# Attention with pooled levels, then eight gated experts, on one core: unit 0's operands built in place by TensorE, pooling by TensorE, and the experts' weights split during units 4 to 6

## The chip, the cores and the metric

One NeuronCore of a Trainium2 chip runs the whole program. The number that counts is the device time in microseconds (us) of one launch, median of the runs; it is compared with the kernel before on the same chip. Engines are named PE (TensorE), DVE (VectorE), ACT (ScalarE), POOL (GpSimd) and SP (SyncE, which here only issues DMAs).

## The reference, cut to what matters

```python
# x: (B=2, T=1024, C=128); 16 heads of 8; windows of 64 keys; 4 levels of 8 pooled keys
x = x + attention(layernorm(x)) @ W_proj + b_proj
#   qkv = xn @ W_attn + b_attn;  per head: scores against the last 64 keys, and, at each level l,
#   against 8 keys that are means over 8*2^l positions of the block of 64*2^l before;
#   mn = min over the five groups of (max over the group's scores); exp(S - mn);
#   the pooled terms are weighted by 8*2^l; sum over all; divide
x = x + moe(layernorm(x))
#   8 experts: h = x @ W1[e].T + b1[e] (512 wide);  g = h[:256] * sigmoid(h[256:]);  eo = g @ Wo.T + bo
#   out = sum over the two chosen experts of eo * gate
```

## The kernel before

All engines walk one list of steps, `SCHEDULE`, written by `schedule()`; each engine issues, in that order, its part of each step, and semaphores tie them. So a wait on one engine holds back all that stands behind it on that engine, and on no other.

**Units.** Attention runs in eight units (2 batches times 4 groups of 4 heads). A unit has ten slots ("score", u, i): slots 0 and 1 are the scores against pooled keys (8 small matmuls each, 64 columns), slots 2 to 9 those against the window (two matmuls of 256 columns, in two of the eight slots a third of 512 columns that adds the mask). ACT takes the exponent of each slot, DVE masks it, and PE multiplies it into the values in the step "out", three slots later. Between them stand the steps of `beside`: work for the other batch, or for the second part of the kernel.

**The maxima.** exp needs the minimum over the groups of the maxima first. The kernel bounds it by the pooled scores: step "guard" (two times 4 matmuls) computes them, "shift" reduces them and splits the negative shift in two parts, "shiftT" transposes it, and "shift load" sends it by two DMAs from ACT's queue into rows 96 to 103 of `qst` and rows 96 and 97 of `qmk`, from where it takes part in the score matmuls as additional rows. "score" slot 0 waits for both.

**Stacked operands.** q and k are computed in fp32r as a rounded part and a rest (`split3`: hi times hi, hi times lo, lo times hi). One unit's `qst` holds 96 rows (three slots of the group's 32 rows: hi, hi, lo), `kst` the keys (hi, lo, hi), `qmk` the queries masked by head, `pkm` the pooled keys masked by head. They are stacked by DMAs: unit 0 from SBUF (`load_queries(0)`, `load_pooled(0)`, `load_keys(0)`, `load_head_queries(0)`), the later ones from a copy of q, k and the pooled keys in DRAM, which the spills write (`spill_queries`, `spill_pooled`, `spill_keys`). Pooling: DVE sums x over 8, 16, 32 and 64 positions into `xpool`, splits it, and "kp" and "pv" multiply it by the weights; "pv" is moved into `vpool` by 8 instructions of DVE and 8 of ACT. Head columns of `pkm` for unit 0 are made by ACT and DVE from `pks`.

**Experts.** `w1` of each expert (512 KB) is loaded to a staging buffer (three of them), summed by POOL (`whole_w1`), rounded by ACT into `w1T_hi` (the buffer of `qmk[0]`) and its rest written by DVE into `w1T_lo`. All eight "w1" steps stand in unit 7. After unit 7 come 16 x 8 steps "hidden" of three 512-column matmuls each, which end the kernel.

**Keeping PE's clock.** `IDLE` names places at which PE multiplies a buffer of zeros, `still`, to stay busy while it would wait.

Of the kernel before, what the change touches and what calls it, by code (L numbers as in the profile page):

```python
# [42 lines left out]
P = 128  # L43
# [23 lines left out]
C_POOLW = C_BAND + WIN  # L67
C_DEN = C_POOLW + 1
# [1220 lines left out]
```

## Time and profile before

| what | value |
|---|---|
| median of 3 runs | 306.48 us (305.94 to 309.51) |
| the profiled execution's own time | 304.07 us |
| its span in the profile | 301.8 us |
| PE / DVE / ACT / POOL busy | 91% / 63% / 53% / 43% |
| mean granted clock of TensorE | 0.876 of 2.4 GHz |
| stages (first score of each unit on PE) | unit 0 at 37.5 us, 1 at 61.9, 2 at 83.2, 4 at 117.5, 7 at 161.5, experts from 187.7 |

The stages partition the span, since PE runs through all of them. "PEclk" of a stretch is the mean of the granted clock: 1.00 is 2.4 GHz, 0.50 is 1.2 GHz, a value between is a stretch with both. A fp32 matmul shows as two instructions in the trace, a fp32r one as one.

### The profile page before, as it was taken

Reading aid. Unit: us, or ns where it says so; the run is one execution under the profiler, and the core shown is the slowest. Engines: PE = TensorE matmul, PEld = TensorE weight load, DVE = VectorE, ACT = ScalarE, POOL = GpSimd, SP = SyncE. Lnnn points to the kernel's source line nnn. Section 1 sums busy time; section 2 is a strip of 40 time slices with the busy share of each in tenths; the row PEclk is TensorE's granted clock in tenths of the full one; section 3 lists DMA queues with packets and bytes.
Section 4 is the critical chain, followed back from the end, with each engine's and each line's share of the span. In section 5 each row is a group of like instructions: output and inputs, shape, how many; then the busy total and the mean of one; then the engine's idle time right before and its main releaser. Section 6 shows DMA issues by size and latency. Waiting matters only on the chain.

```text
span 301.8 us, 6664 instructions
## 1 busy us (share of the span) xinstructions
PE 275.2 (91%) x2380; PEld 226.4 (75%) x2380; DVE 189.7 (63%) x515; ACT 159.5 (53%) x325; POOL 130.5 (43%) x217
## 2 busy tenths in 40 slices
PE   8673789579999899999999997999999999999994
PEld 6452688378788789887888876768888777888883
DVE  7953447705774641544754478677877888778773
ACT  8629262122655637663376374734485655555551
POOL 6200103501312010211250791487788388888882
PEclk9997665755899669999899558999999999999999
DMA  7137765322177654444225670100000000000000
GB/s 223 40 87 239 246 206 131 94 62 38 28 258 240 219 145 118 97 125 102 54 75 157 219 213 21 28 0 18 11 9 11 2 9 18 10 11 9 17 11 17
DMA packets 25215, 27.30 MB, mean 90 GB/s; under 512 B 13056, under 2 KB 19328, under 8 KB 25184
## 3 DMA queue, kind: packets, MB, share of 16 engines
q1 hardware_dynamic: 23840, 25.85, 29.6%
q10 hardware_dynamic: 1344, 1.05, 1.3%
q8 instruction: 19, 0.31, 0.4%
q14 instruction: 12, 0.10, 0.1%
HBM read 15.81 MB, written 7.86 MB: 78 GB/s over the span
## 4 chain that ended last, share of the span: by engine, by line
PE 69%; DVE 10%; ACT 8%; DMA 7%; issue 2%; POOL 1%; SPq 1%; ACTq 1%; DVEq 0%
PE bank L1102 12%; PE bank L1104 11%; PE bank L1103 11%; PE bank L1248 10%; PE bank L1230 6%; PE bank L1218 4%; DMA qmk<-nshiftT 4%; PE bank L1156 3%; DMA w_stage<-w 3%; PE bank L1205 2%; PE bank L1251 2%; PE bank L1227 2%; ACT vpool L426 2%; DVE arena L1058 2%; PE bank L1171 2%
## 5 line engine op out<-in xcount | busy, mean ns | idle before, releaser
L702 POOL TENSOR_TENSOR work<-work 128x256 f32<-128x256 f32 x110 | 80.7, 738 | 27.1 <-DVE work L1085 14.5
L1085 DVE SCALAR_TENSOR_TENSOR work<-bank,comb,work 128x256 f32<-128x256 f32 x128 | 59.2, 481 | 24.8 <-ACT work L834 23.3
L834 ACT ACTIVATE work<-bank 128x256 f32<-128x256 f32 x128 | 48.3, 384 | 44.8 <-PE bank L1104 44.5
L809 ACT ACTIVATE work<-bank 128x512 f32<-128x512 f32 x64 | 37.1, 594 | 39.2 <-PE bank L1230 36.6
L645 POOL COPY vaug<-vwin 128x64 f32<-128x64 f32 x64 | 18.4, 332 | 80.6 <-PE bank L1251 74.5
L1248 PE MATMUL bank<-work,vaug 128*36 128x64 f32 x1024 | 49.7, 251 | 2.7 <-DVE work L1032 2.7
L1248 PEld LDWEIGHTS bank<-work,vaug 128*36 128x36 f32 x1024 | 38.2, 132 | 13.1 <-DVE work L1032 3.8
L1032 DVE TENSOR_TENSOR work<-work,const 128x512 f32<-128x512 f32 x48 | 33.8, 709 | 11.3 <-ACT work L809 11.2
L1230 PE MATMUL bank<-qmk,kst 98*128 98x256 f32 x128 | 35.3, 367 | 0.6 <-ACT work L809 0.6
L1230 PEld LDWEIGHTS bank<-qmk,kst 98*128 98x128 f32 x128 | 26.2, 241 | 4.6 <-issue 1.2
L1102 PE MATMUL bank<-qmk,xT_hi 128*128 128x512 f32 x64 | 27.4, 429 | 0.0
L1102 PE MATMUL bank<-qmk,kst 128*128 128x512 f32 x64 | 26.4, 413 | 0.0
L1103 PE MATMUL bank<-arena,xT_hi 128*128 128x512 f32 x64 | 25.3, 395 | 0.0
L1104 PE MATMUL bank<-qmk,xT_lo 128*128 128x512 f32 x64 | 25.3, 395 | 0.0
L1104 PE MATMUL bank<-qmk,kst 128*128 128x512 f32 x64 | 25.1, 392 | 0.0
L1103 PE MATMUL bank<-arena,kst 128*128 128x512 f32 x64 | 25.0, 391 | 0.0
L1218 PE MATMUL bank<-qst,pkm 104*128 104x64 f32 x128 | 18.5, 298 | 7.0 <-DMA qmk<-nshiftT 6.9
L1218 PEld LDWEIGHTS bank<-qst,pkm 104*128 104x128 f32 x128 | 17.9, 218 | 8.5 <-issue 8.1
L1251 PE MATMUL bank<-work,vpool 128*36 128x64 f32 x256 | 20.9, 248 | 0.0
L621 POOL TENSOR_TENSOR rstd<-veps,nhalf 128x4 f32<-128x4 f32 x8 | 9.3, 1166 | 24.0 <-DVE veps L869 23.9
L1012 DVE TENSOR_REDUCE nshift<-bank 128x16 f32<-128x384 f32 x16 | 8.8, 556 | 16.2 <-PE bank L1156 16.2
L804 ACT ACTIVATE work<-bank 128x512 f32<-128x512 f32 x16 | 9.4, 597 | 17.4 <-PE bank L1218 17.3
(165 smaller groups left out, 481.5 us busy)
## 6 DMA issues: line engine op xcount, KB each, us to landing
w_stage<-w SPq DMA_DIRECT2D x6, 512.0 KB, 4.2
qst<-q_rows SPq DMA_DIRECT2D x7, 384.0 KB, 4.0
qmk<-q_rows SPq DMA_DIRECT2D x28, 96.0 KB
q_rows<-arena SPq DMA_DIRECT2D x2, 1024.0 KB, 5.2
k_rows<-arena SPq DMA_DIRECT2D x2, 1024.0 KB, 4.6
kst<-k_rows SPq DMA_DIRECT2D x7, 256.0 KB, 3.6
pkm<-p_rows SPq DMA_DIRECT2D x28, 48.0 KB
q_rows<-arena SPq DMA_DIRECT2D x2, 512.0 KB, 3.3
```

The costliest lines, as they stand in the source:

```text
L702: gp.tensor_tensor(gacc[t % 2][:, :], gacc[t % 2][:, :], gtmp[(adds - 1) % TMP_RING][:, :], ALU.add).then_inc(acc_done, 1)
L809: act.activation(prob[lo % P_RING][:, :, :, :], bank[sc % SCORE_BANKS][:, :].rearrange("p (c j q) -> p c j q", c=2, j=GH), ACT.Exp).then_i ...
L834: act.activation(sig[hn % SIG_RING][:, :], bank[hn % HID_BANKS][:, HID:2 * HID], ACT.Sigmoid).then_inc(sig_done, 1)
L1032: dve.tensor_tensor(tile, tile, band.unsqueeze(1).broadcast_to([P, 2 * GH, WIN]), ALU.min).then_inc(mask_done, 1)
L1085: dve.scalar_tensor_tensor(dst[:, :], bank[hn % HID_BANKS][:, 0:HID], comb[:, t, e:e + 1], sig[hn % SIG_RING][:, :], ALU.mult, ALU.mult).t ...
L1102: pe.matmul(out, lhs[0], rhs[0], start=start, stop=False)
L1103: pe.matmul(out, lhs[0], rhs[1], start=False, stop=False)
L1104: return pe.matmul(out, lhs[1], rhs[0], start=False, stop=stop)
L1218: ins = pe.matmul(out[:, k * WIN:(k + 1) * WIN], pkm[s][0:SR + 2 * GH, c, :, :].rearrange("p j k -> p (j k)"), qst[s][0:SR + 2 * GH, c * W ...
L1230: ins = pe.matmul(out[:, k * 256:(k + 1) * 256], kst[s][0:SR + 2, c * WIN:c * WIN + P], qmk[s][0:SR + 2, :, c * WIN:(c + 1) * WIN], start= ...
L1248: pe.matmul(o[e], vaug[hu % 2][:, (2 * k + e) % 8, j, :], prob[lo % P_RING][:, e, j, :], start=(j == 0), stop=False)
L1251: ins = pe.matmul(o[e], vpool[u // NG][:, c, u % NG, :], probp[u % 2][:, c, :], start=False, stop=True)
```

## The change

For unit 0 nothing is stacked by DMA any more, but for the masked queries. ACT makes weights whose columns are already repeated for the three slots (`w3_hi`, `wk3`; POOL makes `w3_lo`), so that one `split3` ("qd", "k0") gives `qst` and `kst` of unit 0 in place, and one fp32 matmul ("kd") gives `pks`, for units 0 and 1. The shift of unit 0 is transposed by eight fp32 matmuls ("shiftR") onto the rows at which `qst` needs it; ACT copies it there, and one DMA takes it on to `qmk`. Score slots 0 and 1 of unit 0 wait for these steps alone, and in every unit slot 0 no longer waits for the DMA to `qmk` (now a semaphore of its own, `shift_heads_in`), for which slot 2 waits. Pooling is one step "pl" of eight fp32 matmuls by columns of the constants; `xpool` stays fp32, so "kp" becomes one fp32 matmul and "pv" four steps of 16 fp32 matmuls of 32 x 32 that write all four head groups, each moved by one DVE instruction. q, k, "v" and "kp" of batch 0 move behind unit 0's shift or into unit 0's slots, batch 1's statistics from unit 0 to unit 1, its "v" and "pv" into unit 3. Two of ACT's three copies per "v" go to POOL. The "w1" steps are spread over units 4 to 6 (one in 7), with two staging buffers; the rounded weights go to buffers that are free by then.

```diff
-    s += [("qk", 0, 0, 0), ("qk", 0, 0, 1), ("kp", 0), ("qk", 0, 1, 0), ("qk", 0, 1, 1)]
-    s += [*[("heads", 0, j) for j in range(GH)], ("weight columns",), ("value blanks",), ("v", 0, 0), *[("guard", 0, m) for m in range(2)], ("shift", 0), ("shiftT", 0), ("shift load", 0), ("second buffers",)]
+    s += [("qd", 0), ("kd", 0), ("qd", 1), ("k0", 0), ("k0", 1), *[("heads", 0, j) for j in range(GH)]]
+    s += [("guard", 0, 0), ("guard", 0, 1), ("shift", 0), ("keys lo", 0), ("keys lo", 1), ("qk", 0, 0, 0), ("qk", 0, 0, 1)]
+    s += [("shiftR", 0), ("shiftR", 1), ("shift load", 0)]
...
+        0: {0: [("v", 0, 0)], 1: [("v", 0, 1)], 2: [("kd", 1), ("pv", 0, 0)], 3: [*[("heads", 1, j) for j in range(GH)], ("pv", 0, 1)],
+            4: [("kp", 0)], 5: [("pv", 0, 2)], 6: [("qk", 0, 1, 0)], 7: [("pv", 0, 3)], 8: [("qk", 0, 1, 1)]},
...
+        3: {0: [("pv", 1, 0)], 1: [("pv", 1, 1)], 3: [("pv", 1, 2)], 5: [("pv", 1, 3)], 7: [("v", 1, 0)], 9: [("v", 1, 1)]},
...
+    for i, (u, at) in enumerate([(4, 2), (4, 4), (4, 8), (5, 3), (5, 7), (6, 1), (6, 7), (7, 1)]):
...
-IDLE = {("xT", 0, 0): 20, ("xT", 0, 1): 2, ("kp", 0): 6, ("guard", 0, 0): 6, ("shiftT", 0): 4, ("score", 0, 0): 6}
+IDLE = {("xT", 0, 0): 20, ("guard", 0, 0): 4, ("shiftR", 0): 1, ("score", 0, 0): 2}
...
+                elif kind == "pv":
+                    _, b, m = step
+                    wait_gen_done(pe, ("pl", b))
                     for i in range(4):
+                        keys = xpool[:, 4 * m + i, :, :].rearrange("p l k -> p (l k)")
+                        for j in range(GH):
+                            mine = wqkv[:, 0, 2 * C:3 * C].rearrange("p (g j d) -> p j g d", j=GH, d=DH)[:, j, :, :]
+                            ins = pe.matmul(bk[j * LK:(j + 1) * LK, i * HR:(i + 1) * HR], keys, mine, start=True, stop=True)
...
+                elif kind == "shiftR":
+                    pe.wait_ge(shift_ready, 1)
+                    for i in range(4):
+                        ins = pe.matmul(bk[SR:SR + 2 * GH, i * P:(i + 1) * P],
+                                        nshift_parts[:, :, :, 4 * step[1] + i].bitcast(F32).rearrange("p n j -> p (n j)"), ident, start=True, stop=True)
...
-            load_queries(0)
-            load_pooled(0)
-            load_keys(0)
             load_head_queries(0)
+            load_queries(1)
             spill_queries(0)
+            load_head_queries(1)
             spill_pooled(0)
-            load_queries(1)
-            load_pooled(1)
+            load_keys(1)
             spill_keys(0)
```

PE around unit 0's first score. Before (L1156 is "guard", L1160 "shiftT", L1102 to L1104 a `split3`, here of "v", L1218 slot 0 of the scores):

```order
L1112 MATMUL bank<-still 128x512 x6
L1156 MATMUL bank<-pkm,qst 128x96 x8
L1112 MATMUL bank<-still 128x512 x4
L1160 MATMUL bank<-const,nshift_parts 64x128
L1102 MATMUL bank<-wqkv_hi,xT_hi 128x128
L1103 MATMUL bank<-wqkv_lo,xT_hi 128x128
L1104 MATMUL bank<-wqkv_hi,xT_lo 128x128
...
L1112 MATMUL bank<-still 128x512 x6
L1218 MATMUL bank<-qst,pkm 128x64 x8
```

Now (L1195 is "guard", L1116 to L1118 a `split3`, here of "qk", L1200 "shiftR", L1267 slot 0):

```order
L1126 MATMUL bank<-still 128x512 x4
L1195 MATMUL bank<-pkm,qst 128x96 x8
L1116 MATMUL bank<-xT_hi,wqkv_parts 128x512
L1117 MATMUL bank<-xT_lo,wqkv_parts 128x512
L1118 MATMUL bank<-xT_hi,wqkv_parts 128x512
L1116 MATMUL bank<-xT_hi,wqkv_parts 128x512
L1117 MATMUL bank<-xT_lo,wqkv_parts 128x512
L1118 MATMUL bank<-xT_hi,wqkv_parts 128x512
L1126 MATMUL bank<-still 128x512
L1200 MATMUL bank<-const,nshift_parts 8x128 x8
L1126 MATMUL bank<-still 128x512 x2
L1267 MATMUL bank<-qst,pkm 128x64 x8
```

Behind the guards now stand two `split3` of "qk" and the eight matmuls of "shiftR", where "shiftT" and "v" stood.

SP, the transfers from the first stack to unit 1's. Before:

```order
L462 DMA qst<-arena 32x1024 x3
L462 DMA pks<-kpool 32x512
L462 DMA kst<-arena 32x1024 x3
L462 DMA qmk<-qst 24x1024 x4
L462 DMA q_rows<-arena 128x1024
L462 DMA q_rows<-arena 128x2x1024
L462 DMA p_rows<-kpool 128x512
L462 DMA p_rows<-kpool 128x2x512
L498 DMA qst<-q_rows 96x1024
L513 DMA pkm<-p_rows 24x16x32 x4
L462 DMA k_rows<-arena 128x2x1024
L529 DMA kst<-k_rows 64x1024
```

Now (the second `qst`, `qmk` and `kst` are unit 1's; the last two rows are unit 2's):

```order
L469 DMA qmk<-qst 24x1024 x4
L469 DMA qst<-arena 32x1024 x3
L469 DMA q_rows<-arena 128x1024
L469 DMA q_rows<-arena 128x2x1024
L469 DMA qmk<-qst 24x1024 x4
L469 DMA p_rows<-kpool 128x512
L469 DMA p_rows<-kpool 128x2x512
L469 DMA kst<-arena 32x1024 x3
L469 DMA k_rows<-arena 128x2x1024
L506 DMA qst<-q_rows 96x1024
L514 DMA pkm<-p_rows 24x16x32 x4
```

Unit 0's stacks are gone from the queue but for `qmk`; unit 1's come from SBUF, and unit 2's `pkm` now stands behind `kst` of unit 1.

PE in unit 0, from slot 1 on. Before (L1230 is a window score, L1227 the mask's matmul, L1248 and L1251 the step "out"):

```order
L1218 MATMUL bank<-qst,pkm 128x64 x8
L1230 MATMUL bank<-qmk,kst 128x256 x4
L1227 MATMUL bank<-bar,ident_r 128x512
L1230 MATMUL bank<-qmk,kst 128x256 x4
L1248 MATMUL bank<-work,vaug 36x64 x8
L1251 MATMUL bank<-work,vpool 36x64 x2
```

Now, from slot 2 on (L1284 is a window score, L1281 the mask's matmul, L1157 "kd", L1182 "pv", L1166 "kp", L1304 and L1307 "out"):

```order
L1284 MATMUL bank<-qmk,kst 128x256 x2
L1157 MATMUL bank<-xpool,wk 96x512
L1182 MATMUL bank<-wqkv_sb,xpool 32x32 x16
L1284 MATMUL bank<-qmk,kst 128x256 x2
L1182 MATMUL bank<-wqkv_sb,xpool 32x32 x16
L1281 MATMUL bank<-bar,ident_r 128x512
L1284 MATMUL bank<-qmk,kst 128x256 x2
L1166 MATMUL bank<-xpool,wqkv_sb 128x512
L1284 MATMUL bank<-qmk,kst 128x256 x2
L1304 MATMUL bank<-work,vaug 36x64 x8
L1307 MATMUL bank<-work,vpool 36x64 x2
```

"kd" of unit 1, "kp" and two of the four "pv" now stand between the window scores; further on come the other two "pv" and two `split3` of "qk".

## Rows read from the trace of the kernel before

**Rows 1.** The chain that ended last: start us, us, what

```profile
32.27 5.11 DMA qmk<-nshiftT
...
56.16 5.59 DMA qmk<-nshiftT
...
161.68 4.07 DMA w_stage<-w
```

**Rows 2.** Windows by stage: length; busy of PE, PEld, DVE, ACT, POOL; clock, DMA, GB/s

```profile
0.00:37.50 37.50, 25.05 (x100) 18.36 (x101) 23.39 (x67) 21.89 (x23) 9.03 (x27) 0.86 0.56 168
37.50:61.90 24.40, 18.14 (x156) 15.70 (x156) 14.98 (x45) 8.52 (x18) 6.73 (x7) 0.61 0.50 139
61.90:83.20 21.30, 21.30 (x218) 18.43 (x219) 9.90 (x24) 8.72 (x15) 3.23 (x9) 0.64 0.18 39
83.20:117.50 34.30, 33.54 (x440) 28.51 (x439) 18.25 (x36) 18.94 (x36) 3.55 (x13) 0.85 0.66 199
117.50:161.50 44.00, 44.00 (x652) 36.65 (x651) 22.65 (x58) 26.96 (x51) 9.66 (x30) 0.96 0.37 92
161.50:187.70 26.20, 23.34 (x281) 19.85 (x279) 17.33 (x58) 12.55 (x23) 14.74 (x16) 0.67 0.55 173
187.70:301.80 114.10, 109.84 (x544) 88.91 (x542) 83.19 (x229) 61.88 (x160) 83.56 (x116) 1.00 0.04 12
```

**Rows 3.** Timeline of the first 43 us: start, us, engine line op out<-in [idle before]

```profile
2.49 3.62 ACT L718 ACTIVATE qmk<-zeros 128x4096 fp32r<-128x4096 f32 x1
...
11.21 0.68 DVE L973 TENSOR_TENSOR xT_lo<-bank,xT_hi 128x512 fp32r<-128x512 f32 x1
...
12.04 0.47 PE L1102 MATMUL bank<-xT_hi,wqkv_hi 128*128 128x512 f32 x1 [0.50 <-DVE xT_lo L973]
...
12.58 0.40 PE L1104 MATMUL bank<-xT_hi,wqkv_lo 128*128 128x512 f32 x1
...
21.35 1.74 SPq L462 DMA_DIRECT2D kst<-arena  x3
...
23.01 1.33 ACT L438 ACTIVATE pkm<-pks,const 96x512 fp32r<-96x512 f32 x2 [2.58 <-DMA pks<-kpool]
...
24.49 1.06 PE L1156 MATMUL bank<-pkm,qst 96*128 96x96 f32 x8 [2.67 <-ACT pkm L438]
...
26.49 0.19 DVE L1018 TENSOR_TENSOR nshift_parts<-nshift,nshift_parts 128x32 fp32r<-128x32 f32 x1
...
40.18 2.96 ACT L426 ACTIVATE vpool<-bank,const 32x128 f32<-32x128 f32 x8 [0.97 <-PE bank L1104]
```

**Rows 4.** The same chain, prices on PE; the second and third at clock 0.50

```profile
38.71 0.11 PE bank L1103
...
104.54 0.56 PE bank L1230 x2
105.10 1.01 PE bank L1248 x16
...
119.91 0.86 PE bank L1218 x8
...
126.29 0.43 PE bank L1230 x2
126.72 0.57 PE bank L1248 x16
...
138.42 1.05 PE bank L1164 x2
```

**Rows 5.** DMA issues: KB each, median us from issue to landing

```profile
p_rows<-kpool SPq DMA_DIRECT2D x2, 512.0 KB, 6.1
...
kst<-arena SPq DMA_DIRECT2D x3, 128.0 KB, 3.1
```

**Rows 6.** Unit 7's weights: a group of POOL, and PE's longest wait in the timeline

```profile
L676 POOL TENSOR_TENSOR w_stage<-w_stage 128x512 f32<-128x512 f32 x6 | 8.0, 1341 | 13.6 <-DMA w_stage<-w 13.6
...
185.79 0.64 PE L1248 MATMUL bank<-work,vaug 128*36 128x64 f32 x16 [1.43 <-DVE work L1032]
```

More of the change, by code:

```diff
@@ L66 @@
 C_BAND = C_IDENT + P
-C_POOLW = C_BAND + WIN
-C_DEN = C_POOLW + 1
+C_POOLM = C_BAND + WIN
+POOLC = sum(P // (POOLED << l) for l in range(LEVELS))
+C_VMASK = C_POOLM + POOLC
+C_DEN = C_VMASK + HR
 C_IOTA = C_DEN + GH
@@ L83, in shape_constants @@
     weight = POOLED * 2.0 ** ((np.arange(P) % LK) // POOLED)
-    c[:, C_POOLW] = weight
+    at = C_POOLM
+    for l in range(LEVELS):
+        n = POOLED << l
+        for i in range(P // n):
+            c[i * n:(i + 1) * n, at] = 1.0 / n
+            at += 1
     for j in range(GH):
+        c[j * LK:(j + 1) * LK, C_VMASK + j * DH:C_VMASK + (j + 1) * DH] = weight[:LK, None]
         c[j * LK:(j + 1) * LK, C_DEN + j] = weight[:LK]
@@ L335, in build @@
         still = sb("still", [P, 512], F32R)
+        w1T_hi = [kpool_hi, kpool_lo, wqkv_parts[:, :, :].rearrange("p n c -> p (n c)")[:, 0:2 * HID], still[:, :], pks_whole[:, :]]
+        w1T_hi += [sb(f"w1T_hi{i}", [P, 2 * HID], F32R)[:, :] for i in range(2)] + [qmk[0][:, 0, 0:2 * HID]]
         ident_r = sb("ident_r", [P, P], F32R)
@@ L390, in wait_gen_done @@
         def wait_gen_done(eng, step):
-            kind = step[0] in ACT_LAST
-            n = sum((s[0] in ACT_LAST) == kind for s in GEN[:GEN_AT[step] + 1])
-            eng.wait_ge(gen_act if kind else gen_dve, n)
+            before = GEN[:GEN_AT[step] + 1]
+            if step[0] in APART:
+                eng.wait_ge(k0_done, sum(s[0] in APART for s in before))
+            elif step[0] in ACT_LAST:
+                eng.wait_ge(gen_act, sum(s[0] in ACT_LAST for s in before))
+            else:
+                eng.wait_ge(gen_dve, sum(s[0] not in ACT_LAST and s[0] not in APART for s in before))
         def barred_by_pe(lo):
@@ L952, in _ @@
                 kind = step[0]
-                if kind in GENERAL and kind not in ACT_LAST:
+                if kind in GENERAL and kind not in ACT_LAST and kind not in APART:
                     bk = gen_bank(step)
                     (wait_gen_hi if kind in ACT_FIRST else wait_gen_full)(dve, step)
-                if kind == "weights":
-                    weights()
-                elif kind == "weight columns":
-                    weight_columns()
-                elif kind == "second buffers":
-                    second_buffers()
-                elif kind == "stat":
+                if kind == "stat":
                     _, b, n = step
@@ L1267, in _ @@
                     rows = slice(PAD + (t % TT) * P, PAD + (t % TT + 1) * P)
-                    ins = split3(bank[hn % HID_BANKS][:, :], tuple(x[:, rows] for x in x2T[b]), (w1T_hi[:, e, :], w1T_lo[:, e, :]))
+                    ins = split3(bank[hn % HID_BANKS][:, :], tuple(x[:, rows] for x in x2T[b]), (w1T_hi[e], w1T_lo[:, e, :]))
                     ins.then_inc(hid_full, 1)
```

399 lines of the change are left out of this document (220 added, 179 removed).

## The prediction

> **What bounds the kernel now.** Read the windows by stage first [rows 2]. The last 114.1 us, the experts, are PE at full clock, and the change touches nothing in them. The 187.7 us ahead are what is at stake, and they come in stages: 37.5 us until unit 0's first score, then the eight units. From 61.9 us on PE is busy nearly throughout, but look at the clock: 0.61 and 0.64 in units 0 and 1, 0.85 in units 2 and 3, 0.67 in unit 7. So there are two kinds of loss, waiting at the start and slow matmuls later.
>
> The chain of waits [rows 1] names the waiting: 5.11 us for the shift's transfer ahead of unit 0, 5.59 us for the same ahead of unit 1, and transfers of the experts' weights in unit 7. The timeline of the start [rows 3] adds that ACT waited 2.58 us for `pks` before unit 0's head columns, that the guards began at 24.49 us, and that ACT spent 2.96 us on "pv" in unit 0 while its exponents waited.
>
> The prices come from the chain on PE [rows 4]. At full clock a window slot is 0.43, its "out" 0.57 and a quarter more for the pooled part, 0.7; at the low level they are 0.56 and 1.01 (1.26). A slot and its "out" are thus 1.13 against 1.82 us: each us spent at 1.2 GHz loses 0.38. Slots 0 and 1 are 0.86 each. A fp32 product of 512 columns is 1.05. A `split3` on 128 columns is three times 0.11, one on 512 columns 0.8 (0.27 from the start of one matmul to that of the next [rows 3], three times). A plain unit at full clock is 2 x 0.86 + 8 x 0.43 + 0.4 for two masks + 8 x 0.7 + 1.06 for its guards [rows 3] + 0.3 = 12.5 us.
>
> **The start, to unit 0's first score.** The zero fill of `qmk[1]` on ACT (3.62 us [rows 3]) now stands behind the splitting of the weights; it ends just before the first eviction of x transposed, so that `xT_lo` still begins at about 11.2 us. From there: its 0.68; five small DVE copies of the pooled means at 0.19 to 0.3, 1.0, while it holds the second half of x back; that half 0.68, to 13.6. PE meanwhile makes "qd", then "kd" 1.05 from 12.9, then "qd", "k0", "k0" at 0.8, to 16.4. ACT evicts the last stack (0.6) and makes two head products (1.33), to 18.2: the guards start 6.3 us earlier than 24.49. From there to the split shift 2.2 us, as before (24.49 to 26.68 [rows 3]), to 20.4. The two `split3` of "qk" lie in that time. "shiftR" is eight fp32 products of 128 columns, 1024 columns in all, 2.1; ACT's copy of its second half 0.6: **23.1 us against 37.5, 14.4 less.** What hides the first transfer now: nothing waits for it but slot 2, some 5 us later. The reason is that the 5.11 us transfer, ACT's fills and copies, and `pks` by DMA are all off the path.
>
> **Unit 0.** It takes on what stood ahead: "v" 24 x 0.11 = 2.6, "kd" and "kp" 2.1, two `split3` of "qk" 1.6, and four "pv". No row shows a 32 x 32 fp32 matmul. The nearest is "out": 16 instructions in 0.57, 0.036 each. A "pv" step is 32 instructions: 1.15 us. From above, each could cost the 0.11 of a matmul with a full weight load: 3.5 a step; from below, if its four column groups run side by side where "out" has two, half: 0.6. I take 1.15, since the tile is nearest to that of "out": 4.6. With slots (5.6), five "out" (3.5), guards 1.1 and 0.7 for hand-overs this is 21.8 us at full clock, to **44.9**. "pv" on ACT is gone, and DVE's four moves of 512 elements at 0.68, as its subtraction [rows 3], are 2.7 us, so no engine but PE bounds the unit (DVE was busy 15 us of it before [rows 2], and gives the statistics and normalising of batch 1 to unit 1).
>
> The Trainium skill bears on "pv" (TensorEngine Tiling, Instruction Overhead): a matmul has some 60 cycles of overhead, and a tiling factor should not be taken from a dimension that is already small. By that an instruction of 32 columns costs 60 cycles, 0.025 us at 2.4 GHz, and a step of 32 some 0.8 us; the eight steps would be 2.8 us less than by my row. No run so far shows it.
>
> **Unit 1.** The wait for the shift (5.59) goes, as slot 0 asks only for the first of the two DMAs. Two waits are late next, both on SP's queue. `kst` of unit 1 is copied from SBUF after the last "qk" of slot 8: PE is done with it at 43.7, ACT takes 0.6 and DVE 0.64 [rows 3] and a mask may be ahead, SP issues three at 0.58 [rows 3] to 47.2, and the last lands 3.1 after its issue [rows 5]: 49.8. PE wants it at 46.7: 3.1 us of waiting. Unit 2's `pkm` stands behind that and the spill of the keys, five issues and a landing further: 53.7, while its guard is due at 50.9: 2.8 us. Both can be 0 if unit 0 is slower than I say. After them the clock has fallen, as it did after the wait ahead of unit 1 before (0.64 over the whole unit [rows 2]). The rest of the unit is 12.1 at full clock, "pl" (16 instructions at 0.11) and a transposition included, and I take 9.5 us of it at the low level, 3.5 lost. Sum: 1.7 + 3.1 + 1.1 + 2.8 + 12.1 + 3.5 = 24.3, to **69.2 against 83.2**.
>
> **Units 2 and 3.** A plain unit each, and in unit 2 four `split3` (3.2), "kp" (1.05) and a transposition (0.7): 17.4; in unit 3 four "pv" (4.6) and two "v" (2.6): 19.7. The spill of the pooled keys of batch 1 (6.1 us to landing [rows 5]) now starts in slot 5 and `pkm` of unit 4 waits for it: 1 us of waiting in unit 3, 0 to 3. The sparse "pv" makes a fall of the clock in unit 3 as likely as it was (0.85 over both units): 2.5 lost. 40.6 against 34.3, to **109.8**. A part of the gain is given back here, since 4.6 us of "pv" replace 1.3.
>
> **Units 4 to 6.** "v" of slot 0 of unit 4 is gone (-1.3). Seven "w1" steps come in: POOL 1.34 each [rows 6], ACT and DVE some 0.7 by their 512-element work in [rows 3], PE nothing. POOL (9.7 of 44 us busy) and DVE (22.7) have room [rows 2]; ACT has least, and waits in line for POOL's sum, with the exponents behind it. The three score banks give about three slots of slack. I charge 1.0 (0 to 3): 43.7, to **153.5**.
>
> **Unit 7.** The chain goes through the weights, but PE was behind it by little: PE was busy 23.34 of 26.2 us, at clock 0.67 [rows 2], and its longest wait was 1.43 [rows 6]. Without seven "w1" steps those waits go, 2.9 us; the small matmuls of the gate, which stand where the clock fell, stay. I add 2.0 for a clock that returns sooner: 21.3, to **174.8**. The experts add 114.1: a span of 288.9; 2.3 around it as in the profiled execution (304.07 against 301.8) and 2.4 from there to the median shown (306.48): **294 us**.
>
> **The rivals.** *The clock holds.* Dense work is now spread through units 0 to 3, and the two waits of unit 1 are short. If TensorE stays at 2.4 GHz there and in unit 7, the 3.5 and 2.5 go and unit 7 is 4.5 shorter: 283 to 284. Against it: unit 7 fell to 1.2 GHz without any long wait. *The transfers land late.* Unit 1's two waits and unit 3's are each 2 to 3 us longer, and the clock stays low behind them: 6 to 8 us more, 301. For it: the DMA share is 0.50 and 0.66 in these stages, and the spills of 1 MB stand between. *Slower than before: PE at 1.2 GHz from the first score on.* Unit 0 now has more PE work than any other, and its "pv" feeds little of the array. At the low level unit 0 is some 35 us, unit 1 24, unit 2 27 and unit 3 22; with 43.7, 23.3 and 114.1 behind the start of 23.1 this is 312, with the 4.7 around it 317. It decides from about 35 us at the low level beyond my forecast (13.5 / 0.38). Against it: the start's wait of 3 us that brought the clock down before unit 0 is gone. *It does not do what it says*: the start is held by something else, most likely by POOL, whose two copies of 2048 elements into `pkm` no row shows. At the price of its sum of 512 elements, 1.34 [rows 6], each takes 5.4, and the first, which slot 0 waits for, ends by 18; at twice that the first score comes near 26, 3 us later: 297.
>
> **How the numbers follow.** My forecast (with the last rival's 3 us in it) 0.52, the clock holds 0.24, late transfers 0.16, slower 0.05, other 0.03. The forecast alone spans 287 to 299 by the bounds of "pv", of the waits and of the median. With half of each neighbour the range is **279 to 304**. 2% of 306.48, about what a measurement of this kernel can tell, is 300.4 and 312.6: faster by more 0.80, within 0.15, slower 0.05.
>
> **What would show it.** In the new profile: the guards of unit 0 at about 18 us and the first score at 23; "pv" steps of 1.15 us; unit 1's first score at 45 with waits of some 3 us before its first window slot (for `kst`) and before unit 2's guard (for `pkm`); unit 4 at about 110; unit 7 of 21 us with no wait on DVE. It is wrong if the clock row reads 0.5 through unit 0, if ACT stands waiting for POOL in units 4 to 6 while PE waits for exponents, or if the first score comes after 27 us.

## The result, and the profile after

The changed kernel took 313.16 us (median of 4 runs, 312.12 to 313.31), the kernel before 306.21 us on the same chip: 1.024 times as long, 95% interval 1.019 to 1.028. I had predicted 294. The profiled execution took 312.12 us, with a span of 310.3 and a mean granted clock of 0.89. Some runs of a kernel come out more than 1.5% above its fastest, at a lower mean clock; every ratio, and every median called "like for like", leaves these runs out on both sides, while a plain median counts all.

The windows by stage of the changed kernel, with the first scores as borders (start, units 0, 1, 2, 3, 4, 5, 6, 7, experts), have the columns of [rows 2], with the number of instructions in brackets:

```profile
0.00:25.66 25.66, 21.58 (x95) 15.68 (x96) 18.48 (x55) 15.91 (x20) 14.11 (x27) 0.93 0.37 94
25.66:45.08 19.42, 17.33 (x306) 14.15 (x305) 10.87 (x21) 10.48 (x19) 3.84 (x12) 1.00 0.47 169
45.08:68.76 23.68, 18.45 (x223) 15.82 (x224) 11.31 (x38) 7.53 (x13) 8.92 (x16) 0.71 0.62 159
68.76:85.92 17.16, 16.27 (x224) 13.31 (x223) 9.68 (x22) 10.00 (x18) 2.04 (x8) 1.00 0.20 55
85.92:117.62 31.70, 22.41 (x359) 19.31 (x356) 10.05 (x18) 7.84 (x14) 2.33 (x6) 0.68 0.68 215
117.62:141.97 24.35, 18.39 (x205) 15.40 (x205) 6.22 (x12) 9.16 (x16) 7.72 (x17) 0.58 0.41 104
141.97:160.07 18.10, 17.59 (x228) 13.95 (x224) 13.07 (x23) 8.20 (x15) 4.42 (x7) 0.91 0.53 145
160.07:179.90 19.83, 15.94 (x215) 13.33 (x211) 11.15 (x33) 11.86 (x25) 9.73 (x21) 0.83 0.41 111
179.90:196.38 16.48, 15.87 (x283) 13.77 (x279) 10.84 (x51) 7.86 (x15) 0.76 (x4) 1.00 0.06 12
196.38:310.30 113.92, 109.56 (x546) 88.90 (x542) 83.93 (x229) 61.85 (x160) 83.47 (x116) 1.00 0.04 12
```

Unit 2 begins at 68.8, 14.4 us earlier than before; I had predicted 69.2. Unit 4 begins at 117.6, where it began before: unit 3 alone takes 31.7 us, of which PE works 22.4. Units 4 to 6 then take 62.3 us against 44.0 in [rows 2]; unit 7 gives 9.7 back. So the loss sits in two places, and in both PE does not work at first and works slowly after.

The chain that ended last in the changed kernel (start us, us, what) shows both:

```profile
86.75 7.19 DMA p_rows<-kpool
93.96 0.85 SPq L514
...
96.53 2.53 DMA pkm<-p_rows
99.19 1.06 PE bank L1195 x4
...
127.47 0.76 POOL vaug L635 x4
128.24 1.23 POOL w_stage L699
129.49 0.64 ACT kpool L819
...
131.15 0.55 DVE nshift L1026
...
133.35 0.39 PE bank L1204
```

And the table of waits (engine and line, what it waited for: us in all, times, longest):

```profile
PE bank L1195 <- DMA pkm<-p_rows: 12.9, 2, 9.3
...
PE bank L1204 <- DVE nshift_parts L1032: 11.7, 5, 6.0
...
ACT kpool L819 <- POOL w_stage L699: 8.7, 1, 8.7
```

First place: the guard of unit 4, in slot 2 of unit 3, waits 9.3 us for `pkm` (L1195). SP's timeline of the changed kernel tells why it came so late:

```profile
68.11 3.05 SPq L543 DMA_DIRECT2D qmk<-q_rows  x4
...
83.26 0.70 SPq L553 DMA_DIRECT2D dcomp<-denom  x1
84.01 0.57 SPq L554 DMA_DIRECT2D attT<-denom  x1
84.62 1.06 SPq L469 DMA_DIRECT2D q_rows<-arena  x2
85.73 2.46 SPq L469 DMA_DIRECT2D p_rows<-kpool  x2
```

From 71.2 to 83.3 SP issues nothing. The two rows that end this are `gather_outputs(1)`, which waits for unit 1's normaliser, and ACT was done with that at 83.2; the change put the gathering ahead of the spills of batch 1, so both spills go out together at 84.6 and 85.7, although the pooled keys were ready at 81.4.

Second place: PE stands for 5.96 us ahead of L1204, unit 5's "shiftT". Read the chain's second half backwards: "shiftT" needs DVE's maxima (L1026), which stand behind DVE's part of "w1", that behind ACT's (L819; ACT waits 8.7 us, with its exponents queued behind), that behind POOL's sum (L699), and POOL's sum behind its copy of values (L635). This copy is for unit 4's second half and may start only when the last "out" of unit 3 is done, in slot 4 of unit 4, two slots after the "w1" that stands behind it. The same line stops PE in unit 6 for 3.9 us, where the sum stands behind the statistics.

### The profile page after: what moved, and what is told of

It is laid out like the page before. It is cut to its first block, busy times and chain, and to the rows that moved or that the text cites. A ratio compares the mean times of both kernels' runs of the same rounds, so it can differ in the third digit from the quotient of the medians.

```text
span 310.3 us, 7216 instructions
## 1 busy us (share of the span) xinstructions
PE 273.4 (88%) x2656; PEld 223.6 (72%) x2656; DVE 185.6 (60%) x495; ACT 150.7 (49%) x310; POOL 137.4 (44%) x233
## 4 chain that ended last, share of the span: by engine, by line
PE 72%; DVE 10%; DMA 6%; issue 3%; ACT 3%; SPq 3%; POOL 2%; DVEq 0%; ACTq 0%
PE bank L1116 12%; PE bank L1118 11%; PE bank L1117 11%; PE bank L1304 11%; PE bank L1284 6%; PE bank L1195 3%; PE bank L1267 3%; DMA p_rows<-kpool 2%; PE bank L1307 2%; DMA pkm<-p_rows 2%; PE bank L1249 2%; PE bank L1281 2%; SPq L514 2%; DMA xres<-x 1%; PE bank L1215 1%
## 5 line engine op out<-in xcount | busy, mean ns | idle before, releaser
L871 ACT ACTIVATE work<-bank 128x256 f32<-128x256 f32 x128 | 48.3, 384 | 44.6 <-PE bank L1118 42.7
L1304 PE MATMUL bank<-work,vaug 128*36 128x64 f32 x1024 | 49.0, 249 | 0.6 <-DVE work L1046 0.6
L635 POOL COPY vaug<-vwin 128x64 f32<-128x64 f32 x64 | 14.1, 266 | 77.3 <-PE bank L1307 77.1
L1304 PEld LDWEIGHTS bank<-work,vaug 128*36 128x36 f32 x1024 | 37.7, 131 | 10.8 <-issue 4.0
L1046 DVE TENSOR_TENSOR work<-work,const 128x512 f32<-128x512 f32 x48 | 36.1, 761 | 8.8 <-ACT work L846 8.6
L1284 PE MATMUL bank<-qmk,kst 98*128 98x256 f32 x128 | 35.5, 364 | 1.6 <-DMA kst<-arena 1.6
L1284 PEld LDWEIGHTS bank<-qmk,kst 98*128 98x128 f32 x128 | 25.8, 233 | 6.3 <-issue 2.4
L1195 PE MATMUL bank<-pkm,qst 96*128 96x96 f32 x64 | 12.5, 331 | 14.1 <-DMA pkm<-p_rows 12.9
L1195 PEld LDWEIGHTS bank<-pkm,qst 96*128 96x128 f32 x64 | 10.9, 240 | 16.1 <-issue 15.2
L1026 DVE TENSOR_REDUCE nshift<-bank 128x16 f32<-128x384 f32 x16 | 8.8, 553 | 22.0 <-PE bank L1195 22.0
L1307 PE MATMUL bank<-work,vpool 128*36 128x64 f32 x256 | 20.6, 246 | 0.0
L614 POOL TENSOR_TENSOR rstd<-veps,nhalf 128x4 f32<-128x4 f32 x8 | 8.6, 1075 | 20.7 <-DVE veps L906 20.6
L1267 PE MATMUL bank<-qst,pkm 104*128 104x64 f32 x128 | 16.3, 277 | 1.6 <-DMA qst<-nshiftT 1.6
L1267 PEld LDWEIGHTS bank<-qst,pkm 104*128 104x128 f32 x128 | 15.3, 192 | 2.2 <-ACT work L846 1.7
L699 POOL TENSOR_TENSOR w_stage<-w_stage 128x512 f32<-128x512 f32 x8 | 11.0, 1378 | 12.0 <-DMA w_stage<-w 12.0
L1117 PEld LDWEIGHTS bank<-arena,kst 128*128 128x128 f32 x64 | 12.1, 189 | 1.9
```

The source lines that it names most:

```text
L871: act.activation(sig[hn % SIG_RING][:, :], bank[hn % HID_BANKS][:, HID:2 * HID], ACT.Sigmoid).then_inc(sig_done, 1)
L1046: dve.tensor_tensor(tile, tile, band.unsqueeze(1).broadcast_to([P, 2 * GH, WIN]), ALU.min).then_inc(mask_done, 1)
L1117: pe.matmul(out, lhs[0], rhs[1], start=False, stop=False)
L1195: ins = pe.matmul(bk[:, i * GK:(i + 1) * GK], qst[u % 2][0:SR, t * P:(t + 1) * P], pkm[u % 2][0:SR, 2 * t, :, POOLED:LK], start=True, stop ...
L1267: ins = pe.matmul(out[:, k * WIN:(k + 1) * WIN], pkm[s][0:SR + 2 * GH, c, :, :].rearrange("p j k -> p (j k)"), qst[s][0:SR + 2 * GH, c * W ...
L1284: ins = pe.matmul(out[:, k * 256:(k + 1) * 256], kst[s][0:SR + 2, c * WIN:c * WIN + P], qmk[s][0:SR + 2, :, c * WIN:(c + 1) * WIN], start= ...
```

## The experiments

The time of one variant differs by up to 6% from run to run, and the mean granted clock goes with it (302.15 us at 0.903 and 319.94 us at 0.855 in the first variant); so medians are given with their span, and the verdict on a mechanism is read from its stage of the profile. There is one profile of each variant, so a stretch at a low clock in one of them can be the run's and not the edit's. "Before" is always the kernel before on the same chip in the same session.

**w1 back in unit 7.**

```diff
-    for i, (u, at) in enumerate([(4, 2), (4, 4), (4, 8), (5, 3), (5, 7), (6, 1), (6, 7), (7, 1)]):
+    for i, at in enumerate([1, 1, 2, 3, 4, 6, 7, 9]):
...
-STAGES = 2
+STAGES = 3
```

The loads of "w1" on SP and the third staging buffer also go back to what they were.

> The changed kernel with all eight "w1" steps back in unit 7, in the slots and with the three staging buffers and the loads of the kernel before; all else stays. Theory (a wait in POOL's line): in units 4 to 6 ACT and DVE stand behind POOL's sum of w1, which itself stands behind copies that wait for PE; units 4 to 6 took 62.4 us (first score 117.8 to 180.2) against 44.0 before. Then units 4 to 6 take 44 to 48 us and unit 7 some 26 again instead of 17: 313 less 16 plus 9 is 306 us, range 301 to 308. Rival (the clock alone is low there, whatever stands in the slots): units 4 to 6 stay above 55 us and the time goes up by unit 7's 9 us, to 320.

Median 308.61 us (302.15 to 319.94, 10 runs), before 305.98 (13 runs); like for like 304.10 (3 runs) against 305.39 (9 runs), ratio 0.998 (0.988 to 1.008), so no difference from the kernel before. Windows of this variant: unit 3, units 4 to 6, unit 7.

```profile
87.66:118.05 30.39, 21.63 (x359) 18.71 (x356) 9.98 (x18) 7.86 (x14) 2.33 (x6) 0.66 0.62 190
118.05:162.08 44.03, 44.03 (x639) 36.34 (x638) 22.64 (x58) 24.38 (x46) 10.37 (x32) 0.92 0.36 92
162.08:188.40 26.32, 23.49 (x283) 19.91 (x279) 17.60 (x58) 12.48 (x23) 15.04 (x16) 0.68 0.55 172
```

Units 4 to 6 are back at 44.0, with PE busy throughout: 18.3 us less. Unit 7 costs 9.8 more. The rival, that the clock would be low there anyway, falls (it is 0.92); spreading w1 as the change does is a net loss of 8.4 us in these stages.

**The spills of batch 1 ahead of unit 1's outputs again.**

```diff
                 if u == NG - 2:
-                    gather_outputs(u - 1)
                     spill_queries(1)
                     spill_pooled(1)
...
-                elif 0 < u < UNITS - 1:
+                if 0 < u < UNITS - 1:
                     gather_outputs(u - 1)
```

> The changed kernel with SP's gathering of unit 1's outputs behind the spills and loads of batch 1 again, as in the kernel before; all else stays. Theory (SP's order): the spill of q was issued at 84.6 only because SP stood from 71.2 to 83.3 in front of unit 1's outputs; the pooled keys were ready at 81.4. The spill of p then starts some 4 us earlier and finds no spill of q beside it, and the 9.3 us wait of unit 3's guard shrinks to 3 or 4: 307 us (303 to 310). Rival (the transfers' own length: 7.2 us of spill, 3.3 of issues, 2 of landing, from a product that now stands in slot 5): the wait stays above 7 us and the time above 311.

Median 308.49 us (301.80 to 308.72, 4 runs), before 305.98; like for like only the 301.80 is left, against 305.39. The profile is of a run of 308.47. SP's timeline of this variant:

```profile
83.66 0.83 SPq L469 DMA_DIRECT2D q_rows<-arena  x2
89.35 0.81 SPq L469 DMA_DIRECT2D p_rows<-kpool  x2
...
93.64 3.25 SPq L514 DMA_DIRECT2D pkm<-p_rows  x4
...
97.53 0.70 SPq L553 DMA_DIRECT2D dcomp<-denom  x1
```

and its windows of units 2 and 3:

```profile
71.55:93.87 22.32, 22.32 (x224) 18.42 (x223) 9.64 (x22) 10.11 (x18) 2.04 (x8) 0.69 0.43 149
93.87:111.58 17.71, 16.72 (x359) 14.51 (x356) 9.79 (x18) 7.85 (x14) 2.60 (x6) 1.00 0.59 164
```

Unit 3 takes 17.7 us instead of 31.7, and the guard's wait is 0.97: better than the 3 to 4 expected. The spill of q is out 5.7 us ahead of that of p, and from p's issue to `pkm`'s it is now 4.3 us (89.35 to 93.64) where it was 8.2 (85.73 to 93.96). So the wrong order cost twice: a later start, and two spills beside each other. But a good third of the gain is missing in unit 2, 22.3 us at clock 0.69 with PE never idle, where the changed kernel had 17.2 at 1.00.

Such a slow unit 2 gives the spill more time, so it is a rival for the short wait. Two other profiles rule it out. With the old order and a unit 2 just as slow (22.3 us, "Zeros in unit 3's wait" below) the gap ahead of the guard is still 9.3 us. With the new order and a unit 2 as fast as the changed kernel's (the variant "Everything" without zeros, below) unit 3 takes 17.6:

```profile
65.87:83.03 17.16, 16.27 (x223) 13.29 (x223) 9.66 (x22) 9.99 (x18) 2.03 (x8) 1.00 0.60 207
83.03:100.59 17.56, 16.76 (x360) 14.54 (x356) 9.88 (x18) 7.86 (x14) 2.58 (x6) 1.00 0.60 164
```

There p's spill is issued 12.6 us after the unit's start instead of 17.0, and `pkm` 4.2 us behind it instead of 8.2: 8.4 us together, and the guard's wait is 0.8 us instead of 9.3.

**Only the pooled product earlier**, to tell SP's line from the later slot of "kp".

```diff
-        2: {0: [("xT", 1, 1)], ... 5: [("kp", 1)], ...
+        2: {0: [("kp", 1), ("xT", 1, 1)], ...
```

> The changed kernel with the product of batch 1's pooled keys in slot 0 of unit 2, where the kernel before has it, instead of slot 5; SP's order stays the changed one, with unit 1's outputs ahead of the spills. Theory (SP's line decides): the spills still start at some 84 us and unit 3's guard waits 8 to 9 us: 313. Rival (the later slot of the product decides): the wait falls below 4 us, and the time to 306.

Two runs, 314.17 and 317.33 us, before 301.79. SP's timeline of this variant:

```profile
86.85 0.57 SPq L554 DMA_DIRECT2D attT<-denom  x1
87.46 1.06 SPq L469 DMA_DIRECT2D q_rows<-arena  x2
88.57 2.26 SPq L469 DMA_DIRECT2D p_rows<-kpool  x2
```

The guard still waits 8.8 us. The slot of the product is not the cause; SP's line is.

**Both edits.** The first two together.

> Both edits at once: "w1" back in unit 7 and the spills of batch 1 ahead of unit 1's outputs. If both theories hold and the two places are apart, the gains add: 313 less 7 less 6 is 300 us (295 to 303), the part of the change's start that is kept. If the clock ties them together (one wait's low clock leads to the next), it is lower than the sum, 295. If both rivals hold, it is over 313.

Median 297.09 us (292.19 to 299.79, 4 runs), before 305.98; like for like 293.84 (2 runs) against 305.39. Windows of this variant: units 3, 4 to 6, 7.

```profile
91.23:108.83 17.60, 16.73 (x359) 14.52 (x356) 9.79 (x18) 7.85 (x14) 2.60 (x6) 1.00 0.60 165
108.83:152.90 44.07, 44.07 (x639) 36.46 (x638) 22.66 (x58) 24.39 (x46) 10.37 (x32) 0.92 0.39 99
152.90:179.75 26.85, 23.56 (x283) 20.02 (x279) 18.05 (x58) 12.48 (x23) 14.90 (x16) 0.68 0.52 169
```

Stage by stage the two gains add: unit 3 is 14.1 us shorter than in the changed kernel, units 4 to 6 18.2, and unit 7 10.4 longer. Against the kernel before the median is 8.9 us less, 11.6 like for like, where neither edit alone made a difference that these runs can tell (2.6 and 2.5 us more, like for like 1.3 and 3.6 less): without the two lines of waits the rest of the change is worth some 9 to 12 us.

**POOL's late copy behind the first two sums.** The narrowest cut of the second place.

```diff
-                    if hu + 2 < 2 * UNITS and hu + 2 != UNITS and hu + 2 != UNITS + 1:
+                    if hu + 2 < 2 * UNITS and hu + 2 != UNITS:
                         values_of(hu + 2)
...
-                        values_of(UNITS + 1)
```

> The changed kernel; only POOL's copy of the values for unit 4's second half, which waits for the end of unit 3's "out" (slot 4 of unit 4), goes from unit 3's slot 9 to unit 4's slot 6, so behind the first "w1" steps instead of ahead of them. Theory (a wait in POOL's line): PE's idle 5.96 us ahead of unit 5's shift goes, and part of the low clock from 119.7 to 139 us with it: 6 to 9 us less, 305 (303 to 308). Rival ("w1" itself, ACT's and DVE's 0.6 and 0.7 us and POOL's 1.3 each, is too much beside a unit): the wait stays at 4 us or more and the time above 311.

Median 313.00 us (306.51 to 315.82, 4 runs), before 305.98; like for like only the 306.51 is left, against 305.39. Windows of units 4 and 5 of this variant (a run of 312.08):

```profile
119.65:134.68 15.03, 15.03 (x206) 12.63 (x205) 6.57 (x12) 9.19 (x16) 7.83 (x17) 0.77 0.70 174
134.68:159.87 25.19, 25.19 (x228) 19.30 (x224) 12.33 (x23) 8.09 (x15) 3.97 (x7) 0.59 0.38 105
```

At its place the theory holds wholly: unit 4 takes 15.0 us instead of 24.4, PE is never idle, with the same "w1" in it. Unit 6's wait of 3.9 us, which this edit does not touch, is still there. On the whole the gain does not show: unit 5 takes 25.2 instead of 18.1, busy throughout, at 0.59. Whether that low stretch follows from the edit or from the run I can't say; the time moved by no more than its spread.

**The same, with ACT's and DVE's part two slots behind POOL's sum**, and the spills first.

```diff
-        beside.setdefault(u, {}).setdefault(at, []).append(("w1", i))
+        beside.setdefault(u, {}).setdefault(at, []).append(("w1 sum", i))
+        later = 10 * u + at + 2
+        beside.setdefault(later // 10, {}).setdefault(later % 10, []).append(("w1", i))
```

> Spills first, and "w1" in units 4 to 6 as in the changed kernel, but unhooked: POOL's sum stays in its slot, ACT's and DVE's parts come two slots later, and POOL's late copy of values stands behind the first sum. Theory (waits in line, not the work of w1): no wait of PE for the shift in units 4 to 6, 44 to 48 us for the three, unit 7 at 16 to 18 us where the kernel with w1 in unit 7 and spills first had 26.9: 288 us (285 to 296) against its 297. Rival (the work beside the units lowers the clock or fills ACT and DVE anyway, as unit 5 took 25.2 us at clock 0.59 once unit 4's wait was gone): units 4 to 6 stay above 54 us, and the time is 300 or more.

Median 296.44 us (292.21 to 306.46, 4 runs), before 304.30; like for like 292.27 (2 runs) against 303.81. Windows of units 4 to 6 and of unit 7:

```profile
107.35:159.96 52.61, 50.02 (x639) 41.12 (x639) 27.96 (x65) 28.49 (x53) 22.23 (x44) 0.81 0.55 150
159.96:176.44 16.48, 15.87 (x282) 13.76 (x278) 11.35 (x52) 8.50 (x16) 0.77 (x4) 1.00 0.06 12
```

Neither side of the expectation holds alone. The 6.0 us wait is gone and one of 2.6 in unit 6 is left, yet units 4 to 6 take 52.6, not 44 to 48: PE is busy 50.0 of it, at 0.81 where w1 in unit 7 gives 0.92. With unit 7 the four take 69.1 us, with w1 in unit 7 70.9. But one profile each does not settle it: the unhooked kernels below took 74.4 and 78.4 for the four. A gain of the spread is not shown. Unit 3, with no wait of PE's for `pkm`, took 21.2 us here, at 0.76.

**Unit 1's waits by order alone** (w1 in unit 7, spills first): SP loads unit 2's queries and pooled keys ahead of unit 1's keys, unit 1's guards one slot earlier.

```diff
-GUARD_AT = [5, 2, 2, 2, 2, 2, 2]
+GUARD_AT = [4, 2, 2, 2, 2, 2, 2]
...
             spill_pooled(0)
+            load_queries(2)
+            load_pooled(2)
             load_keys(1)
```

> w1 in unit 7 and spills first (297 us), and unit 1's waits attacked by order alone: SP loads unit 2's queries and pooled keys ahead of unit 1's keys, and the guards of unit 1 stand one slot earlier in unit 0. Theory: the 3.8 us wait for unit 2's pooled keys and the 1.6 us for unit 1's shift go, the clock falls later or less in units 1 and 2 (0.66 and 0.76, 46.5 us together): 290 us (285 to 295). Rival: SP stands in front of the landing of the pooled spill, unit 1's keys come later, and the wait only changes its name: 296 or more.

Median 291.21 us (288.37 to 296.66, 4 runs), before 304.30; like for like 288.87 (2 runs) against 303.81. The waits for unit 1's shift (1.6) and for `pkm` (3.8) are gone; the one for `kst` grew from 1.55 to 3.05, as the rival said, over a quarter of what went. Unit 1 is 22.0 us at 0.77 instead of 25.1 at 0.66, and unit 2 20.3 instead of 21.4. Some 3 us more of this profile's gain lie in unit 4, which the edit does not touch: 12.1 us at clock 1.00, where the same instructions had taken 15.1 at 0.77.

**Zeros in unit 1's waits**: 26 products that do nothing, and the waits stay as they were (w1 in unit 7, spills first).

```diff
-        ("score", 0, 0): 2}
+        ("score", 0, 0): 2, ("score", 1, 0): 6, ("score", 1, 2): 6, ("guard", 2, 0): 14}
```

> w1 in unit 7 and spills first (297 us), and 26 products of zeros on PE in the three places of unit 1 where it waits (6 ahead of slot 0, 6 ahead of slot 2, 14 ahead of unit 2's guard), the waits themselves left. Theory (the waits cost more by the clock that falls behind them than by their own length): unit 1 runs near clock 1.00 and takes 19 to 21 us instead of 25.1, unit 2 17.2 instead of 21.4: 288 us (285 to 292). Rival (the clock falls there for another reason, and the products only delay what follows): 297 or more.

Median 293.61 us (286.86 to 299.05, 4 runs), before 304.30; like for like 287.57 (2 runs) against 303.81. Windows of units 1 and 2 of this variant:

```profile
45.04:65.71 20.67, 19.37 (x244) 16.02 (x244) 10.38 (x38) 7.43 (x13) 9.34 (x16) 1.00 0.68 178
65.71:84.38 18.67, 17.78 (x223) 14.47 (x222) 9.66 (x22) 9.98 (x18) 2.03 (x8) 0.91 0.57 192
```

The clock stays at 1.00 through unit 1, and the unit takes 20.7 us instead of 25.1, waits included. This is more than one run's chance: in all three profiles with zeros in unit 1 its clock is 1.00, and in the ten others of the changed kernel and its variants it is 0.65 to 0.77. In the eight of these ten with the same waits in unit 1 the unit took 23.7 to 25.1 us, and units 1 and 2 together 40.8 to 47.4, where they take 39.3 here.

**Zeros in unit 3's wait**, in the changed kernel as it is: the price of the clock apart from that of the wait.

```diff
-        ("score", 0, 0): 2}
+        ("score", 0, 0): 2, ("guard", 4, 0): 40}
...
+                if step == ("guard", 4, 0):
+                    pe.wait_ge(norm_done, 2)
```

> The changed kernel with 40 products of zeros on PE while it waits for unit 4's pooled keys in unit 3; the wait of 9.3 us itself stays. It prices the clock apart from the wait. Theory (what the wait brings down costs as much again): unit 3, 31.7 us at 0.68, takes 17.5 plus 9.3, 27 us, and unit 4 gains nothing certain: 308 us (304 to 311). Rival (the clock is no part of it): 313.

Median 310.60 us (309.56 to 312.50, 4 runs), before 301.79; ratio 1.033 (1.025 to 1.041). This lies between the theory's 308 and the rival's 313. Windows of units 2 and 3 of this variant:

```profile
71.36:93.67 22.31, 22.31 (x223) 18.41 (x222) 9.63 (x22) 10.10 (x18) 2.03 (x8) 0.69 0.13 34
93.67:119.68 26.01, 25.99 (x399) 21.96 (x396) 9.79 (x18) 7.85 (x14) 2.59 (x6) 1.00 0.67 211
```

Unit 3 is 26.0 us at 1.00 instead of 31.7 at 0.68: 5.7 us less, with the gap as long as before (9.3 us, now filled with zeros). That these 5.7 us are the price of the clock behind the wait is not shown, though. This profile's unit 2, which the edit does not touch, ran at 0.69 and took 5.2 us longer than the changed kernel's, and units 2 and 3 together took 48.3 us, against 48.9 in the changed kernel and 47.5 to 47.6 in the three other profiles that have the wait and no zeros in it. The two low stretches go by turns in the other profiles too. Unit 3 ran at 1.00 in all six in which unit 2 ran below 1.00, this one among them. Of the seven in which unit 2 ran at 1.00, unit 3 was low in six: at 0.66 to 0.71 in the four with the wait, and at 0.76 (21.2 and 21.4 us) in two without it. So it may be that the clock falls once in these two units wherever the wait stands.

**Everything, with w1 unhooked and with w1 in unit 7.** First without the zeros:

> The unhooked w1 in units 4 to 6, spills first, and unit 1's loads in the new order, together. If each theory holds, 288 less 7: 281 us (277 to 290), the best of all. If the unhooked w1 costs what it did, 295 or more.

Median 293.41 us (290.71 to 307.61, 4 runs), before 304.30, like for like 290.93 (2 runs) against 303.81: not the 281 expected. Its unit 7:

```profile
153.35:174.95 21.60, 21.60 (x282) 18.89 (x278) 11.59 (x53) 8.60 (x16) 0.77 (x4) 0.68 0.04 9
```

The same instructions as in the 16.48 us above, PE busy without a gap, at clock 0.68: that is 5.1 of the 9.7 us by which the profiled run missed 281. Most of the rest is the 4 us by which the unhooked kernel alone, at 292, had missed its own 288.

Then with the last three sums later, the keys' products of unit 0 in slots 5 and 6, and 8 products of zeros ahead of unit 1's slot 2:

> The unhooked w1 in units 4 to 7 (its last three sums later: unit 6 slot 5, unit 7 slots 0 and 2), spills first, unit 2's loads ahead of unit 1's keys, the products for unit 1's keys in slots 5 and 6 of unit 0, and 8 products of zeros ahead of unit 1's slot 2. Units 4 to 7 took 69 to 74 us with w1 unhooked and 69 to 71 with w1 in unit 7. Theory (the 2.6 us wait of unit 6 is POOL's line once more, behind the statistics): that wait goes, units 4 to 7 take 66 us, and the time is 284 us (279 to 291). Rival (spread over the units w1 gives nothing, since the clock there, 0.62 and 0.82 in units 4 and 6, takes back what unit 7 gains): no better than the same kernel with w1 in unit 7.

> The same edits to units 0 and 1 and to the spills, with w1 in unit 7 as in the kernel before. Against the kernel with the new order alone (291 us): unit 1's remaining wait of 3.05 us for its keys shrinks to 1 or 2 with their products earlier, and the zeros hold the clock across it (1.00 instead of 0.77 in unit 1, 0.83 in unit 2): 284 us (281 to 290). Rival (moving the products only moves the wait, and the clock falls somewhere else): 290 or more.

Median 288.54 us (284.16 to 295.97, 5 runs) with w1 unhooked, ratio to before 0.948 (0.938 to 0.958); 289.48 us (284.60 to 294.21, 4 runs) with w1 in unit 7, ratio 0.961 (0.949 to 0.973). Before took 301.79. Like for like these are 285.55 and 286.03 (2 runs each) against 300.71. Windows of units 1 and 2 with w1 in unit 7:

```profile
44.20:61.52 17.32, 16.40 (x235) 13.88 (x232) 11.68 (x39) 7.45 (x14) 9.31 (x16) 1.00 0.62 175
61.52:80.17 18.65, 17.76 (x223) 14.46 (x222) 9.66 (x22) 9.98 (x18) 2.03 (x8) 0.91 0.62 202
```

and of units 4 to 6, and of unit 5 alone, with w1 unhooked (the profile is of the slowest of its five runs, 295.97 us):

```profile
101.83:157.30 55.47, 54.81 (x639) 44.39 (x638) 27.68 (x60) 26.50 (x50) 22.62 (x43) 0.72 0.46 122
119.11:144.31 25.20, 25.20 (x227) 19.32 (x223) 10.80 (x26) 7.95 (x15) 4.43 (x8) 0.59 0.47 128
```

Unit 1, 25.1 us once both faults were mended, is 17.3, and PE works 16.4 of it. Unit 6's wait for the shift is gone too in the unhooked kernel (its unit 6 is 13.0 us), so the theory held there; but its profiled execution has a unit 5 of 25.2 us at 0.59. Which of the two ways of placing w1 is better stays open: the intervals overlap. Both beat the kernel before and the changed one.

## Why the prediction was wrong

Its steps beside what the profiles measured, in us. The last column is the variant with both faults mended.

| step | predicted | changed kernel | both mended |
|---|---|---|---|
| start | 23.1 | 25.7 | 25.3 |
| unit 0 | 21.8 | 19.4 | 19.5 |
| unit 1 | 24.3 | 23.7 | 25.1 |
| units 2 and 3 | 40.6 | 48.9 | 39.0 |
| units 4 to 6 | 43.7 | 62.3 | 44.1 |
| unit 7 | 21.3 | 16.5 | 26.9 |
| experts | 114.1 | 113.9 | 114.0 |
| span | 288.9 | 310.3 | 293.7 |

**The step that failed first: "`pkm` of unit 4 waits for it: 1 us of waiting in unit 3, 0 to 3."** It was 9.3, and unit 3 was 14.0 us longer than with the spills first; 8.3 of this is PE standing still and 5.7 its working at a lower clock, and whether the second part belongs to the wait is open. I saw the spill of p come from slot 5 and priced that; I did not follow what the change put ahead of the spills on SP's queue. In the kernel before, the gathering ahead of the spills was unit 0's, over by 81.8, and 12.4 us were left from q's issue (86.55) to unit 3 (98.92); in the changed kernel 1.3 us were left. The variants with the spills first and with the product early settle it.

**The step that cost most: "ACT ... waits in line for POOL's sum ... I charge 1.0 (0 to 3)".** Units 4 to 6 were 18.3 us longer than with w1 back in unit 7: PE stood still for 10.4 of it and worked at a lower clock for the rest (0.75 over the three units, against 0.92). How much of that rest the waits brought is not shown, since unit 5 fell to 0.59 without any. The line was named, but I counted its slack in ACT's queue alone ("The three score banks give about three slots of slack"). What mattered is what stood ahead of the sum in POOL's queue: a copy that waits for PE, which soon waited for ACT and DVE. The price of "w1" itself was right (POOL 1.23 to 1.71 us, ACT 0.6, DVE 0.7), and with the one copy moved unit 4 was 15.0 us. The sign to look for stood in the prediction ("if ACT stands waiting for POOL in units 4 to 6 while PE waits for exponents"), but as a warning, not as a price; and PE waited for the shift, which DVE makes, not for exponents.

**Terms that were mis-sized, without weight for the sign.** The start was 2.6 longer: the clock fell near 14 us, "kd" took 1.91 us instead of 1.05, and ACT's copies of `kst` (1.28) stood ahead of the head products, so the guards began at 20.55 and not at 18.2. POOL's two copies into `pkm` took 3.85 together, not 5.4 each, and held nothing. The wait for unit 1's shift did not go, as I wrote, but shrank from 5.22 to 1.62 (the 5.59 of [rows 1] is the transfer's own time). The wait for `kst` was 1.6 (predicted 3.1), for `pkm` 3.65 (2.8). Unit 7, 16.5 against 21.3, ran at clock 1.00 in this profile; in another variant the same unit took 21.6 at 0.68.

**"pv"** took 0.46 us a step, not 1.15, as the timelines of unit 0 of the changed kernel show (start, us, what):

```profile
31.34 0.46 PE L1182 MATMUL bank<-wqkv_sb,xpool 128*32 128x32 f32 x32
31.73 0.50 PE L1284 MATMUL bank<-qmk,kst 98*128 98x256 f32 x2
```

32 instructions in 0.39 us to the start of the next. That is below even my lower end: four steps are 3.0 us less than I took, and unit 0, with the 1.6 us wait for unit 1's shift at its end, came out 2.4 shorter. A part of the error is in the row that I scaled: its 0.57 for "out" is the chain's, and from its start to the next start "out" takes 0.47. By the rule that the prediction quotes (the Trainium skill, TensorEngine Tiling, Instruction Overhead) it would be 0.8 us; the trace does not agree, it is half of that.

**What was right:** where the start's gain comes from and that it reaches unit 2 (68.8 against 69.2), that two transfers are late next in unit 1, and roughly the size of the whole without the two lines: 288.9 of span forecast, 293.7 measured. There is luck in both numbers. That unit 2 began on time is an error of 2.6 us in the start set off by one of 2.4 in unit 0; and the 293.7 are those of a kernel with w1 in unit 7, which was not the one forecast. With w1 spread and unhooked, and the spills first, the span was 290.4, with other errors in its stages.

The rival "the transfers land late" named unit 3's wait, but gave it 2 to 3 us more and not 8, and by the length of the transfers, not by what stands ahead of them. The slow outcome had been given one mechanism, a clock at 1.2 GHz from unit 0 on, and the clock in unit 0 was 1.00. Its sum is also too low by the prediction's own price (1 us becomes 1 / 0.62): unit 2's 17.4 would be 28 and not 27, and unit 3's 19.7 would be 32 and not 22. And to the kernel before it was 12.5 us, not 13.5. Neither bears on the outcome.

## What to carry to other kernels

A step that is moved must be followed through every in-order queue it passes, and the question is not how long the thing ahead of it takes but what that thing waits for: here 1.3 us of issues on SP and a 0.8 us copy on POOL made unit 3 14 us and unit 4 9 us longer, because each waited for something that follows from PE's own progress. Split a step that three engines share, so that the first engine's part stands ahead of any instruction that waits for PE, and the last one's a slot or two behind. And look at the clock behind a wait of PE, not only at its length: products of zeros in unit 1's waits made the unit 3.0 to 4.4 us shorter here, with the waits still in it. For unit 3's wait such a gain is not shown.

## What the runs showed of the hardware

- The granted clock fell in stretches in which PE had no gap at all: unit 5 took 25.2 us with PE busy 25.2, at 0.59, in two variants, and some 16.0 at 1.00 in others, with the same instructions on PE (busy as the profile counts it, which does not say how full the array was); unit 7 took 21.6 at 0.68 and 16.5 at 1.00. The Trainium skill (TensorE: Matmul & The Clock Gate, What's actually happening) has the gate follow how busy PE has been; the waits of unit 1 agree (1.00 in three profiles with zeros, 0.65 to 0.77 in ten without), these two units do not show it. What else brings it down stays open. Such a fall can hide the removal of a wait: with POOL's copy moved, unit 4 became 9.3 us shorter, and unit 5, at 0.59 in that run, 7.1 longer.
- Two spills beside each other: the last part of the pooled keys' spill took 7.19 us in the chain with the spill of q issued 1.1 us ahead of it. In the five profiles with that order `pkm` was issued 8.2 to 8.4 us after p's spill; in the eight with 4.7 to 5.7 us between the spills it was 4.1 to 4.3 us.
- fp32 products of 32 x 32, written to four column groups, went through at 0.39 us for 32 instructions, 12 ns each, where 16 instructions of "out" take 0.47 by the same measure, from start to next start, 29 ns each.
